# In 30 steps of layer A TensorE turns the second head's probabilities through the side bank and VectorE copies them; the experts' tokens are counted late in their step

## The reference, cut to what matters

```
x = x + tanh(g0) * attention_A(context, norm(x))      # 8 heads of 64, 487 keys
x = x + tanh(g1) * experts(norm(x))                   # 8 experts, the best 2 of each token
x = x + tanh(g2) * attention_B(context, norm(x))      # 16 heads of 64
x = x + tanh(g3) * ffn(norm(x))                       # quantised, with a convolution of 3
```

## Time and profile before

| | us |
|---|---|
| median of 3 runs | 1475.03 |
| lowest, highest | 1464.38, 1475.82 |
| the profiled execution | 1461.97 |
| its span | 1460.2 |
| steps 5 to 32 in it | 69.98 to 282.10 |

### The profile page before, as it was taken

One profiled execution on the slowest core, in us unless ns is written; L12 is line 12 of the kernel. 1 busy time (PEld: TensorE's weight loads), 2 busy tenths in 40 slices (PEclk: granted clock), 3 DMA queues, 4 the chain that ended last, 5 costly groups with the idle time before them and its releaser, 6 DMA issues.

```text
span 1460.2 us, 45515 instructions
## 1 busy us (share of the span) xinstructions
PE 1254.3 (86%) x16920; PEld 985.2 (67%) x16920; DVE 1066.5 (73%) x2851; ACT 971.2 (67%) x2319; POOL 1097.7 (75%) x1346
## 2 busy tenths in 40 slices
PE   1888878779999888777999999899999999999863
PEld 0566656558777766656888888677777777777652
DVE  5777768966666678786666667778878878888655
ACT  2887768566566667554656565777778777778741
POOL 5887768687677665455777767798888988888763
PEclk9989899989999999989999999999999999999995
DMA  7689997689999969359999998455454455445420
GB/s 249 156 187 228 193 192 178 137 202 232 255 250 253 263 125 216 89 120 211 249 262 248 250 253 213 102 103 108 100 101 99 99 105 100 99 95 107 78 62 7
DMA packets 450620, 239.99 MB, mean 164 GB/s; under 512 B 390000, under 2 KB 424672, under 8 KB 448096
## 3 DMA queue, kind: packets, MB, share of 16 engines
q1 hardware_dynamic: 417912, 178.51, 60.1%
q10 hardware_dynamic: 29416, 51.22, 10.9%
q0 software_dynamic: 3072, 7.34, 1.8%
HBM read 107.78 MB, written 35.50 MB: 98 GB/s over the span
## 4 chain that ended last, share of the span: by engine, by line
PE 46%; ACT 12%; DVE 10%; DMA 8%; issue 8%; POOL 8%; DVEq 3%; SPq 3%; ACTq 2%; POOLq 0%
PE bank_ring L1152 9%; PE bank_ring L1138 8%; PE bank_ring L1190 7%; DMA probs_turned<-probs 5%; PE bank_scores L1112 5%; PE bank_out L1171 4%; PE bank_x L1204 3%; PE bank_x L1253 3%; ACT scores L908 3%; PE bank_x L1125 2%; DVE scores L1419 2%; ACT probs L915 2%; POOL probs L700 2%; ACTq L1053 2%; ACT values L935 2%
## 5 line engine op out<-in xcount | busy, mean ns | idle before, releaser
L700 POOL TENSOR_TENSOR probs<-scores,probs 112x487 f16<-112x487 f32 x373 | 412.3, 1122 | 193.2 <-ACT probs L915 187.5
L908 ACT ACTIVATE scores<-scores,score_min 112x487 f32<-112x487 f32 x384 | 266.0, 694 | 159.7 <-DVE score_min L1419 158.5
L915 ACT ACTIVATE probs<-scores 112x487 f16<-112x487 f32 x384 | 214.1, 604 | 38.6 <-DMA probs_turned<-probs 22.7
L1419 DVE CUSTOM_DVE_ANT_0 scores<-bank_scores,mask 112x487 f32<-112x487 f32 x384 | 238.2, 657 | 0.9 <-PE bank_scores L1112 0.7
L1152 PE MATMUL bank_ring<-weights,kv_B 128*128 128x128 f16 x3072 | 195.6, 221 | 1.7 <-DVE keys L1436 1.7
L1152 PEld LDWEIGHTS bank_ring<-weights,kv_B 128*128 128x128 f16 x3072 | 184.7, 99 | 10.8 <-DVE keys L1436 2.7
L1171 PE MATMUL bank_out<-values,probs_turned 128*128 128x64 f16 x4608 | 169.9, 194 | 23.2 <-DMA probs_turned<-probs 14.1
L1441 DVE SCALAR_TENSOR_TENSOR values<-bank_ring,values 128x512 f16<-128x512 f32 x192 | 132.1, 688 | 77.7 <-ACT values L935 73.3
L1138 PE MATMUL bank_ring<-kv_B,weights 128*128 128x488 f16 x768 | 180.0, 371 | 0.0
L935 ACT ACTIVATE values<-bank_ring 128x512 f16<-128x512 f32 x192 | 112.2, 585 | 99.7 <-PE bank_out L1171 98.6
L1171 PEld LDWEIGHTS bank_out<-values,probs_turned 128*128 128x128 f16 x4608 | 157.3, 99 | 27.8 <-DMA probs_turned<-probs 14.6
(11 more groups left out here) (236 smaller groups left out, 2458.0 us busy)
## 6 DMA issues: line engine op xcount, KB each, us to landing
expert_up<-experts_up SPq DMA_DIRECT2D x86, 512.0 KB, 5.3
expert_down<-experts_down SPq DMA_DIRECT2D x43, 512.0 KB, 5.6
raw_weights<-in_weights ACTq DMA_DIRECT2D x8, 1536.0 KB, 11.0
experts_up<-expert_up ACTq DMA_DIRECT2D x8, 1024.0 KB, 5.2
probs_turned<-probs SPq DMA_TRANSPOSE x384
context_turned_B<-kv_B ACTq DMA_DIRECT2D x16, 375.0 KB, 8.7
kv_B<-context_turned_B ACTq DMA_DIRECT2D x16, 375.0 KB, 3.7
moe_results<-moe_result SPq DMA_DIRECT2D x43, 128.0 KB, 4.9
```

What stands on the lines that cost most here:

```text
L700: pool.tensor_tensor(PR[:, u % 4, 1, 0:KEYS], S[:, u % 4, 0:KEYS], PR[:, u % 4, 0, 0:KEYS], ALU.subtract).then_inc(probs_split[u % 2], 1)
L908: act_e.activation(S[:, u % 4, 0:KEYS], S[:, u % 4, 0:KEYS], ACT.Exp, bias=rmin[:, u % 4:u % 4 + 1], scale=-1.0, accum_out=rsum[:, g % 2, ...
L915: act_e.activation(PR[:, u % 4, 0, 0:KEYS], S[:, u % 4, 0:KEYS], ACT.Copy).then_inc(probs_ready, 1)
L1419: dve.tensor_tensor_reduce(out=S[:, u % 4, 0:KEYS], in0=bS[u % 2][0:TOK, 0:KEYS], in1=mask[:, m, 0:KEYS], scale=1.0, scalar=3.0e38, op0=AL ...
```

## The change

1. Heads u = 2j + 1 with j from 4 to 33 are no longer sent through the DMA transpose. `early(j)` begins with a task `s_turn` for u = 2j - 1, in steps 5 to 34: TensorE waits for the remainder of that head and turns the tile in eight pieces of 112 x 128 into the side bank, read as f16; VectorE copies 128 x 896 f16 from there to `probs_turned`. The task takes its place in the order of the side bank, ahead of the step's other early tasks.
2. `sum_values` waits for that copy, and ScalarE's rounding of head u + 4 for TensorE's filling, where they waited for the transfer.
3. The task `route` moves from `early` to the end of `late` in its step; `place_rows` moves on VectorE from ahead of the keys' remainder to the end of the step; `weigh_experts` comes three steps later.

```diff
 def early(j):
     tasks = []
+    if turned_by_pe(2 * j - 1):
+        tasks.append(("s_turn", 2 * j - 1))
...
-    for b in range(2):
-        if j == routed(b) + 2:
-            tasks.append(("route", b))
...
 def late(j):
...
+    for b in range(2):
+        if j == routed(b) + 2:
+            tasks.append(("route", b))
     return tasks
...
+TURN_STEPS = range(4, 34)
+
+
+def turned_by_pe(u):
+    return u % 2 == 1 and u // 2 in TURN_STEPS
...
-                    turn_probs(2 * j + 1)
+                    if not turned_by_pe(2 * j + 1):
+                        turn_probs(2 * j + 1)
...
             def round_probs(u):
                 if u >= 4:
-                    act_e.wait_ge(turned[(u - 4) % PT_BUFS], turns_done(u - 4))
+                    if turned_by_pe(u - 4):
+                        act_e.wait_ge(x1_filled, X1_AT[("s_turn", u - 4)])
+                    else:
+                        act_e.wait_ge(turned[(u - 4) % PT_BUFS], turns_done(u - 4))
...
-                    pe.wait_ge(turned[u % PT_BUFS], turns_done(u))
+                    if turned_by_pe(u):
+                        pe.wait_ge(x1_drained, X1_AT[("s_turn", u)])
+                    else:
+                        pe.wait_ge(turned[u % PT_BUFS], turns_done(u))
...
-                if name == "p_turn":
+                if name == "s_turn":
+                    pe.wait_ge(probs_split[1], n // 2 + 1)
+                    for i in range(8):
+                        last = pe.transpose(bX1h[:, TOK * i:TOK * i + TOK],
+                                            PR[:, n % 4, i // 4, 128 * (i % 4):128 * (i % 4) + 128], idh[0:TOK, 0:TOK])
+                    last.then_inc(x1_filled, 1)
+                elif name == "p_turn":
...
+                if name == "s_turn":
+                    dve.wait_ge(values_summed, n - PT_BUFS + 1)
+                    dve.tensor_copy(PT[n % PT_BUFS][:, 0:8 * TOK], bX1h[:, 0:8 * TOK]).then_inc(x1_drained, 1)
...
-                    if j == routed(b) + 2:
-                        place_rows(b)
-                    if j == routed(b) + 3:
+                    if j == routed(b) + 6:
                         weigh_experts(b)
...
                 if m[2]:
                     gate_hidden(m[2][1], m[2][2], m[2][3])
+                for b in range(2):
+                    if j == routed(b) + 2:
+                        place_rows(b)
```

More of the change, by code:

```diff
@@ L490, in turns_done @@
         def turns_done(u):
-            return 16 * (u // PT_BUFS + 1)
+            return 16 * sum(not turned_by_pe(v) for v in range(u % PT_BUFS, u + 1, PT_BUFS))
         block = stack.enter_context(nc.Block())
@@ L1825, in _ @@
                 for t in late(j):
-                    part(t)
+                    if t[0] != "route":
+                        part(t)
                 if halves_in_step(j):
```

## The result

Slower, and by twice what was forecast. The kernel before has a median of 1472.32 us over four runs beside it (1464.38 to 1475.82), the changed kernel 1517.05 us over four (1508.90 to 1529.06); the ratio is 1.0321, 95% interval 1.0276 to 1.0366. That is 45 us more, where the sum had 22.9. The profiled execution took 1521.29 us, its span is 1519.5 us.

The account below looks back on a forecast made before the run. VectorE was taken to pace steps 5 to 32, TensorE leading by some 4 us. Six cycles 30.9, a seventh 3.1 and two copies 1.1 made 35.1, less 12.2: 22.9 us slower, 1475.03 to 1498 us; range 1468 to 1522.

Parts of the forecast that it names:

- the falling clock: Rival: TensorE idling before the heads' turning halves the clock for values and scores, +10 to +20 us more, 1508 to 1518; chance 0.15.
- The bank wait decides: Side bank: TensorE's next task waits for VectorE's copy, idle 2 to 3 us before the heads' turning in 7 steps.
- Copy 0.63 us: VectorE: copying 128 x 896 f16 from PSUM takes 0.63 us, charged at 0.55 after overlap.
- Turnings 0.6 us and hidden: TensorE: eight f16 turnings a step take about 0.6 us, costing nothing while TensorE leads VectorE by 4 us.
- Transfers, -12.2: Steps 5 to 32: dropping 30 transfers saves TensorE's 12.2 us of waits; about half if first heads become late.
- Counting, 0: Moved token counting and expert weighing: taken as 0 us, with -2 and +2 as ends.
- Later stretches as long as now: Sign of being right: the stretches after steps 5 to 32 keep their length.
- The cycle without a stall, 32 us: Steps 25 to 28, 27.10 us before: expected 32; no longer than 28 would show the forecast wrong.
- 4k+2: These steps pay the copy alone, 0.55 us; the side bank couples, but VectorE waits for ScalarE there anyway.
- 4k+3: These steps, by step 15: heads turn only after VectorE's copy, so the next mask comes 2.6 us later.
- 4k: These steps, by step 16: output projection waits for the copy, structural cost 1.45 us against before without its stall.
- the seventh cycle: Steps 29 to 32: about 3.1 us instead of 5.15, as TensorE can catch up behind VectorE's choice of experts.

Follow-up runs that it names:

- e1_turns_only: Changed kernel with tokens counted and weighed where the kernel before does it, leaving only turnings and copies: 1519.58 us, ratio 1.0364 to before.
- e2_counting_only: Kernel before with tokens counted at the end of their step and experts weighed three steps later, no turning on TensorE: 1467.41 us, ratio 1.0000.
- e6_transfers_out: Kernel before without the 30 second-head transfers and their waits, nothing in their place, output not the reference's: 1459.23 us, ratio 0.9953.
- e8_awake: Turnings-only version of the changed kernel plus 36 unused matmuls behind the turning in all steps but 4k + 1: 1494.03 us, ratio 1.0170 to before.
- e10_token_awake: Kernel before plus a tiny turn and 8-column copy at the 30 places, with 36 unused matmuls behind it except in 4k + 1: 1494.78 us, ratio 1.0125.
- e4_token: Kernel before, all transfers kept, plus one identity-tile turn and an 8-column copy at the 30 places in the side bank: 1501.96 us, ratio 1.0250.

## Why the prediction was right, and where it was short

The direction, the range and the mechanism held; the likeliest number was 22 us too low, and 1517 lies near the upper end of the range (1468 to 1522). It is inside because that end was drawn for a rival, the falling clock, at 1508 to 1518. By its own steps:

- *The bank wait decides*: right. The tiny token at the same places costs 32.5 us by itself, while the copy's time alone costs 3 to 5. TensorE's idle time of 2 to 3 us ahead of the heads' turning is there (2.83 in step 15), and in the expert input's and output projection's place as well.
- *Copy 0.63 us*: 0.614 (median of 30). *Turnings 0.6 us and hidden*: eight in 0.56.
- *Transfers, -12.2*: -13.4 in the stretch, and first heads did not come late in their place.
- *Counting, 0*: ratio 1.0000.
- *Later stretches as long as now*: in the profiled pair the span grew by 59.3 us and the stretch by 49.9, but e1_turns_only, e2_counting_only and e6_transfers_out show that steps far behind vary by several us from one execution to the next (step 76 takes 7.6 us in before, 7.1 in e1_turns_only and 11.7 or more in after, e2_counting_only and e6_transfers_out). So the end agrees with the stretch within 10 us, no better.
- *The cycle without a stall, 32 us*: 34.40.

The step that failed most is the last term, the clock, which I took as 0 in the sum and set aside as a rival of 0.15 with 10 to 20 us. Set a kernel nearly without that loss (e8_awake, where filler keeps the clock up) beside the sum. The forecast priced six equal cycles and a seventh apart, so the four columns by kind are means over the first six cycles, steps 5 to 28, against before, in us:

| | 4k+1 | 4k+2 | 4k+3 | 4k | six cycles | seventh, 29 to 32 | end to end |
|---|---|---|---|---|---|---|---|
| forecast | +0.55 | +0.55 | +2.6 | 1.45 - 12.2/6 = -0.58 | +18.7 | +3.1 | +22.9 |
| e8_awake | +0.61 | +0.47 | +2.64 | -0.68 | +18.2 | +8.2 | +25.6 |
| e1_turns_only | +0.79 | +1.50 | +4.23 | -0.09 | +38.6 | +9.6 | +50.2 |
| after | +0.75 | +1.54 | +4.05 | -0.06 | +37.6 | +12.3 | +44.7 |

In the first six cycles the second row is close to the forecast. Its 4k + 2 shows that the bank's coupling is indeed covered there, as long as the clock stays up. The two rows in the middle differ by the filler alone: 0.2, 1.0, 1.6 and 0.6 us by kind, 20.4 in six cycles, 21.7 in all seven and 25.5 end to end.

How much of this is the change's own? In steps 4k + 2 and 4k + 3 TensorE spends 12.1 us at half clock in before and 47.8 in e1_turns_only. There the low clock came with the change, and there lie 16 of the 21.7 us. In steps 4k before has more of it (22.8 us) than e1_turns_only (13.7), and the filler takes that away too: the 4 us gained there may not be a loss that the change brought. And it is shown only with filler in place of idle time. The heads' turning starts 4.52 us behind the mask with and without it, but step 28 is 1.6 us longer with it (7.33 against 5.71), so it is not free everywhere; a kernel with the wait and the full clock and no filler can't be had.

The fault was twofold. The chance: the earlier trace rows showed a 2.6 us wait of TensorE followed by 0.55 of clock, and I forecast a wait of 2 to 3 us in front of work that I had on the path. After that the fall of the clock was not a rival with a chance of its own, but part of the same case. The size: I charged one step in four with 1.5 to 2 us, and to 3 with the step behind it; it was three steps in four, 3.4 us a cycle. The Trainium skill (TensorE: Matmul & The Clock Gate, A second HAM failure mode: psum-queue depth-cycling) describes a kernel in which TensorE's short pauses between groups of matmuls send the clock up and down and cost throughput. This trace agrees in kind: the pauses are 2 to 3 us for a PSUM bank, and the same 24 matmuls take 1.50 us in one step and 2.37 in another. I had that rule at hand and not in the sum.

The second term that was mis-sized is the seventh cycle, put at 3.1 us because TensorE could catch up behind the choice of experts. It cost 12.3 us in the changed kernel and 8.2 in e8_awake. That kernel's 6.8 us at half clock all lie in its steps 29 and 31, so how these 8.2 divide between wait and clock stays open. The sixth sequence runs a step ahead of the others: its expert input, which stands in a step 4k + 2 for them, comes in step 29, of the kind 4k + 1 that I had down as free of a second early task. So the bank couples where I charged a copy alone, and step 29 takes 10.32 us for 7.07:

```profile
288.59 0.61 DVE L1704 COPY probs_turned<-bank_x 128x896 f16<-128x896 f16 x1
...
289.26 0.63 PE L1260 MATMUL bank_x<-identity_f,x_normed_M 112*128 112x112 f32 x2 [3.50 <-DVE probs_turned L1704]
```

In steps 31 and 32 TensorE did not catch up but waited longest of all for the copy, 4.41 and 4.58 us.

The 0.55 us a step for the copy was right where the bank couples (0.46 to 0.68 at full clock, e8_awake against e10_token_awake), and too much for a copy for which nobody waits.

## What to carry to other kernels

A new task in a shared PSUM bank is priced by what stands behind the *next* user of the bank on TensorE, not by its own microseconds: ask when the engine that empties it comes to it, and put the fill where the empty comes early. Look for that next user in every step: one sequence can have its tasks in other steps than the rest, as here the sixth. When that question gives a TensorE wait as long as those that the trace shows ahead of a low clock (here 2.5 to 3 us), and what stands behind it is on the path, count that work at the half clock in the same sum, not as a separate chance. Where something else came late anyway, raising the clock gained nothing here, and filler matmuls helped only where they started before the wait. And before a stretch of one execution is compared with another, look for one step that a late transfer made long.

## What was not expected of the hardware

- Useless matmuls paid: 36 of 128 columns in each of three steps in four (2.17 us a step) made the kernel 26 us faster, with 2.4 GHz kept (half clock from 68.3 to 6.8 us of 28 steps).
- After a wait of 2.83 us the loss lasts beyond the first group: values 2.37 for 1.50 us, sums 1.49 for 0.86, and the router's four matmuls 0.72 for 0.54.
- The fall does not follow every such wait. In steps 5 to 32 of the changed kernel TensorE waits 2.5 us or more 15 times, and the clock drops during 14 of these waits or within 2.5 us behind them. e4_token waits 2.56 us in the same place of step 15 and its values run at full clock:

```profile
154.08 0.60 PE L1256 MATMUL bank_x<-identity_f,wide 112*128 112x112 f32 x4 [2.56 <-DVE token L1693]
154.52 1.50 PE L1163 MATMUL bank_ring<-weights,kv_A 128*128 128x128 f16 x24
```

  So one step's timeline can show either.
- Eight f16 turnings of 112 x 128 run overlapped, 0.56 us for all, though one is listed with 212 ns.
